# Row sums ahead of the transposed weights' low halves in a pipelined attention loop

## What is computed

```
x = x + cross_attention(layernorm(x), ctx)   # 16 heads of 64, RMS-normed q and k, softmax over 77 keys
x = x + moe0(layernorm(x))                   # 8 experts, top 2, hidden 256
x = x + layernorm(x) @ W1.T + mean(ctx) @ W2.T + b
x = x + moe1(layernorm(x))                   # 8 experts, top 2, hidden 1024
```

## Time and profile before

| what | us |
|---|---|
| median of three runs | 828.95 |
| span of the profiled execution, first to last instruction | 823.7 |
| attention steps 6 to 15, start of q_lo to start of q_lo | 115.63 to 229.83 |
| attention steps 16 to 20 | 229.83 to 279.28 |

### The profile page before, as it was taken

The page is one execution under the profiler, slowest core; times in us unless marked ns, Lnnn a source line. Parts: engine busy times, 40 slices in busy tenths (PEclk is TensorE's granted clock), DMA queues, the critical chain, the costliest instruction groups (busy, mean ns, idle before and its releaser), DMA issues.

```text
span 823.7 us, 16893 instructions
## 1 busy us (share of the span) xinstructions
PE 616.4 (75%) x5984; PEld 543.6 (66%) x5984; DVE 548.4 (67%) x975; ACT 379.5 (46%) x568; POOL 437.0 (53%) x406
## 2 busy tenths in 40 slices
PE   5857889999996516786753552179999999999960
PEld 4646888899985415665642442069998899999850
DVE  3963679999987675686636776936555555555536
ACT  1744267778765315665413666324444433333420
POOL 6563569988886237776418873453333333332120
PEclk9976599999998857889885777579999999999995
DMA  8200002211221305767732322021111121111018
GB/s 281 71 4 27 27 2 65 65 40 60 65 66 65 96 32 185 230 211 214 214 131 83 97 84 61 22 77 39 47 47 53 53 53 52 46 48 33 21 43 301
DMA packets 45168, 70.27 MB, mean 85 GB/s; under 512 B 6113, under 2 KB 34530, under 8 KB 44834
## 3 DMA queue, kind: packets, MB, share of 16 engines
q1 hardware_dynamic: 34786, 42.70, 16.5%
q0 software_dynamic: 8160, 22.29, 9.4%
q10 hardware_dynamic: 2144, 4.19, 1.4%
HBM read 50.81 MB, written 18.35 MB: 84 GB/s over the span
## 4 chain that ended last, share of the span: by engine, by line
PE 45%; DVE 22%; DMA 9%; issue 8%; POOL 8%; ACT 7%; DVEq 1%; SPq 0%; POOLq 0%; ACTq 0%
PE banks L1193 43%; DMA sorted_y<-slot_region 5%; POOL wb_region L556 2%; PE banks L1391 2%; DVE x_res L1120 1%; DVE w_region L886 1%; DVE rs L878 1%; DVE w_region L891 1%; ACT w_region L666 1%; POOL w_region L440 1%; DMA w_region<-token_y 1%; POOL rv L464 1%; DVE slot_region L1025 1%; DVE w_region L1025 1%; ACT w_region L599 1%
## 5 line engine op out<-in xcount | busy, mean ns | idle before, releaser
L1193 PE MATMUL banks<-w_region 128*128 128x128 f16 (+5 forms) x1948 | 177.5, 253 | 31.9 <-POOL w_region L515 12.1
L1193 PEld LDWEIGHTS banks<-w_region 128*128 128x128 f16 (+1 forms) x1948 | 163.1, 127 | 41.7 <-POOL w_region L515 12.4
L1193 PE MATMUL banks<-w_region,wb_region 128*128 (+1 forms) x1168 | 138.6, 278 | 11.8 <-DMA wb_region<-wk 6.7
L1193 PEld LDWEIGHTS banks<-w_region,wb_region 128*128 128x128 f16 (+1 forms) x1168 | 120.0, 106 | 25.8 <-issue 8.0
L566 POOL DMA_INDIRECT token_y<-slot_region,lg x46 | 45.5, 989 | 160.8 <-DVE slot_region L1090 153.8
L1193 PE MATMUL banks<-slot_region,w_region 128*128 128x256 f16 x1104 | 126.4, 275 | 0.0
L728 ACT ACTIVATE wb_region<-wb_region 128x1024 f32<-128x1024 f32 x46 | 48.6, 1057 | 168.0 <-DVE wb_region L1072 168.0
L1193 PEld LDWEIGHTS banks<-slot_region,w_region 128*128 x1104 | 108.2, 99 | 13.0
L524 POOL DMA_INDIRECT slot_region<-normed_rows,index x92 | 94.3, 1025 | 34.2 <-issue 24.5
L1072 DVE SCALAR_TENSOR_TENSOR wb_region<-banks,b_s 128x1024 f32<-128x1024 f32 x46 | 56.2, 1224 | 71.0 <-PE banks L1193 71.0
L1193 PE MATMUL banks<-wb_region,w_region 128*128 (+1 forms) x344 | 57.8, 321 | 31.5 <-DVE slot_region L1090 22.0
(11 more groups left out here) (233 smaller groups left out, 1073.4 us busy)
## 6 DMA issues: line engine op xcount, KB each, us to landing
staging<-w_t SPq DMA_DIRECT2D x32, 512.0 KB, 4.2
sorted_y<-slot_region SPq DMA_DIRECT2D x23, 256.0 KB, 4.7
x_res<-x SPq DMA_DIRECT2D x4, 512.0 KB, 9.3
staging<-w_in SPq DMA_DIRECT2D x8, 256.0 KB, 2.9
normed_rows<-w_region SPq DMA_DIRECT2D x16, 128.0 KB, 1.7
staging<-w_out SPq DMA_DIRECT2D x8, 256.0 KB, 3.0
normed_rows<-wb_region SPq DMA_DIRECT2D x16, 128.0 KB, 1.9
w_region<-token_y ACTq DMA_DIRECT2D x2, 1024.0 KB, 8.8
```

What stands on the lines that cost most here:

```text
L1193: return t.matmul(o, a, b, start=start, stop=stop)
```

## The change

In VectorE's step, `sums(s - 4)` moves from between `pt_lo(s - 5, 1)` and `pt_lo(s - 5, 2)` to ahead of `pt_lo(s - 5, 0)`. No instruction is added, removed or resized, and each keeps its waits.

```diff
                 if 0 <= s - 6 < NT:
                     stats(ln1, s - 6)
+                if 0 <= s - 4 < NT:
+                    sums(s - 4)
                 if 0 <= s - 5 < NT:
                     pt_lo(s - 5, 0)
                     pt_lo(s - 5, 1)
-                if 0 <= s - 4 < NT:
-                    sums(s - 4)
-                if 0 <= s - 5 < NT:
                     pt_lo(s - 5, 2)
                 if 0 <= s - 2 < NT:
                     q_ms(s - 2)
```

## The result

The changed kernel takes 834.51 us (median of four runs, 832.9 to 837.64) against 828.27 us for the kernel before (four runs, 827.33 to 830.36). The ratio is 1.0067, with a 95% interval of 1.0043 to 1.0092: slower by about 0.7%. The prediction said 834.6 us.

The account below looks back on a forecast made before the run. VectorE was busiest, TensorE nearly as full, with chains through group 2 setting step ends. 2.70 + 2.00 + 0.1 + 0 + 0.86 = 5.66 us on a median of 828.95 gave 834.6, range 831.0 to 839.0.

Parts of the forecast that it names:

- The block that moves: VectorE's sums, L878's start to pt_lo 2: keeps its 1.83 us, so pt_lo 0 begins at E + 1.83.
- The wait this opens: TensorE idles some 0.5 us for pt_lo 0; pt_lo 2 starts 1.63 us after pt_lo 0, at E + 3.46.
- E: Start of pt_lo 0 in the old order, the prediction's zero: 187.26 in step 12, 175.88 in step 11.
- An even step: Steps 6, 8, 10, 12, 14: ScalarE's chain from pt_hi 2, and q_lo with it, 0.54 us later; 2.70 in all.
- An odd step: Steps 7, 9, 11, 13, 15: VectorE's pt_lo 2 and all behind it 0.40 us later; 2.00 in all.
- Steps 5 and 16: Step 5 already waits 0.22 us at pt_lo 2, so pays about 0.1; step 16 adds nothing.
- Steps 17 to 19: Step 17 adds nothing; in steps 18 and 19 attn follows pt_lo 2, 0.43 us later each; 0.86 in all.
- Gained: Row sums come 1.20 us earlier, so GpSimd's L487 may start earlier; costed at nothing.
- The first rival: TensorE's clock stays at 2.4 GHz in steps 18 and 19, giving back 3.3 us: 831.3, not slower; chance 0.07.
- The second: Much slower: GpSimd's L482 starts before VectorE's L840, up to 2.25 us in five odd steps, 846 us; chance 0.08.
- The third rival: No change: slack in the steps covers the wait, each costing under 0.2 us, 831 us; chance 0.05.

Follow-up runs that it names:

- e1: Against the kernel before, sums moved one place further back, between the low halves of group 0 and group 1, in every step; ratio 0.9984.
- e6: Changed kernel plus, in even steps, ScalarE's L599 moved ahead of the high half of group 2; 830.65 us beside 829.41 for the kernel before.
- e3: Kernel before with the changed order only in even steps under 16; even steps 12.00 us, odd 11.34, step 5 to add_attn of step 20 168.77.
- e4: Kernel before with the changed order only in odd steps 7 to 15; odd steps 11.80 us, even 11.43, step 5 to add_attn of step 20 168.21.
- e12: The changed kernel run again unaltered, beside the kernel before; ratio 1.0073, interval 1.0043 to 1.0102.
- e11: e9 with sums ahead of group 0, so the changed order plus both the ScalarE and GpSimd moves; 850.25 us beside 825.66 for the kernel before.
- e7: Kernel before, VectorE's old order kept, with ScalarE's L599 moved ahead of group 2's high half in even steps; ratio 1.0014.
- e10: e9 without ScalarE's move: sums between groups 0 and 1 plus GpSimd's L440 moved; 825.66 us beside 825.66 for the kernel before.
- e8: Kernel before with sums between groups 0 and 1 and ScalarE's L599 moved ahead of group 2's high half in even steps; 826.47 us, ratio 0.9956.
- e9: e8 plus GpSimd's L440 moved from the even step's end to behind L482 of the next step; 821.14 us, ratio 0.9948 to the kernel before.
- e2: Kernel before with sums moved behind all three low halves in every step; 863.31 us beside 824.52 for the kernel before.

## Why the prediction was right

It was right in sign and mechanism and near in size; one of its terms was mis-sized. By its own steps:

- *The block that moves:* 1.83 us forecast, 1.86 measured.
- *The wait this opens:* pt_lo 0 to pt_lo 2 in 1.63 us, as read from step 20; pt_lo 2 at E + 3.46 forecast, E + 3.49 measured (179.40 - 175.91). e1 shows that this trip is the cause: with group 0 ahead of the sums the cost is gone.
- *An even step:* 0.54 forecast, 0.55 to 0.60 measured, 2.82 in all against 2.70. That it goes over ScalarE was argued in the prediction; the wait of q_lo for ScalarE (0.60 us in step 12) and e6 show it.
- *An odd step:* 0.40 forecast, 0.40 to 0.44 measured, 2.16 against 2.00. e3 and e4 show that the two kinds of step are paid for separately, 0.52 and 0.41 us a step.
- *Steps 5 and 16:* 0.1 and 0 forecast, 0.14 and 0.00 measured.
- *Steps 17 to 19:* 0, 0.43 and 0.43 forecast, -0.40, 1.37 and 0.47 measured. This is the mis-sized term, 1.44 in place of 0.86. In step 18 the two transposes took 0.69 us and not 0.44, and the 30 matmuls 5.79 and not 5.12; with the 0.43 that makes 1.35. In step 19 the transposes and attn took what they took before, and the 0.43 came out as 0.47. In step 17 they took 3.45 and not 4.79, of which VectorE's own work let 0.40 through. The prediction's sum had held the clock constant; why it fell earlier in step 18 and came back in step 17 stays open.
- *Gained:* nothing forecast. The wait of L487 for the row sums shrank, and nobody waits for L487; measured nothing.

The sum is 6.6 us in place of 5.7 inside the loop. That the median of the times met the forecast to 0.1 us is luck beyond that: the forecast stood on a median of 828.95 for the kernel before, which a fourth run made 828.27, so the difference measured is 6.2 us, and beside the repeat e12 it is 7.0. The 5.25 us that the prediction puts around the span are not that either: the profiled run of the changed kernel took 832.9 us with a span of 831.1, so about 1.8 us lie around a span and the rest is scatter between runs.

The first rival (the clock comes back in steps 18 and 19) did not happen there, and did in step 17, which I had not named. The second (GpSimd shuts VectorE out) did not happen, but the lead shrank as worked out: to 0.35 us, where 0.4 was forecast. Step 11 of the changed kernel:

```profile
183.51 1.22 DVE L840 SCALAR_TENSOR_TENSOR wb_region<-staging,wb_region 128x1024 f16<-128x1024 f32 x1
183.86 2.98 POOL L482 TENSOR_TENSOR w_region<-w_region,rq 128x1232 f32<-128x1232 f32 x1
```

Here L840 was first, and L482 took 2.98 us in place of 2.25: the late one pays, 0.73 us where L840 had 0.87 left. By the rule in the Trainium skill, SBUF — State Buffer, "SBUF: two separate sides", whoever starts first holds the shared ports to its end; this row and the rows of e11 agree, one for each winner. Its chance of 0.08 was for a jump of 11 us that was 0.35 us away. The third rival (the wait is covered) falls: each of steps 6 to 15 is 0.40 to 0.60 us longer, where it needed under 0.2.

## What to carry to other kernels

Before moving an operation in a hand-written order, look for a round trip over other engines that starts and ends on the same engine on either side of it; the operation may be the cover of that trip. A stretch of the same trace where the operation is missing, as in the pipeline's last step, gives the bare length of the trip. Where one bound is removed and nothing comes out, look for a second loop of the same length: shortening ScalarE's chain alone left 22.81 us a pair (e7), shortening GpSimd's loop alone 22.79 (e10), and only shortening both gave anything, 0.4% (e8) and 0.5% (e9).

## What the runs showed of the hardware

Two effects are not linear in the delay. After waits of VectorE had left TensorE's weight loads idle for 2.84 us (e2) and 2.64 us (e11), the granted clock was 0.50 and 0.53, and in e2 the score instructions took 5.89 us in place of 3.20. The kernel e2, expected to cost 10 to 15 us, lost 37 in the loop, some 12 of them by the clock in my estimate. And which of VectorE and GpSimd starts first by a few tenths of a us decides which of them loses: L482 took 2.98 us in the changed kernel, and the pair of norm_lo 2.82 us in place of 0.75 in e11. Against that, steps 8 to 15 of the changed kernel repeat to 0.02 us between its two profiles.
